# Relative-position attention on Trainium2: half a tile's contents made directly behind the turning of two chunks

## The reference

```python
x = x + 0.5 * ffn(layernorm(x))
x = x + attn(layernorm(x))          # below
x = x + 0.5 * ffn(layernorm(x))

# attn, 16 heads of 16, scale = 1 / sqrt(16)
q, k, v = heads(w @ Wq.T), heads(w @ Wk.T), heads(w @ Wv.T)
rp = heads(sin_table(2 * Lq - 1) @ Wr.T)
AC = einsum('bhid,bhjd->bhij', q + u_bias, k)        # contents
BD = rel_shift(einsum('bhid,hjd->bhij', q + v_bias, rp))   # positions
out = einsum('bhij,bhjd->bhid', softmax((AC + BD) * scale), v)
```

## Time and profile before

| | |
|---|---|
| median of 3 runs | 3118.8 us (3118.35 to 3139.53) |
| the profiled execution's own time | 3117.44 us |
| its span, first to last instruction | 3115.6 us |
| mean granted TensorE clock | 0.959 |
| TensorE matmul busy | 2880.4 us, 92% of the span |
| VectorE busy | 2632.4 us, 84% |
| ScalarE busy | 2497.8 us, 80% |
| GpSimd busy | 2310.7 us, 74% |

### The profile page before, as it was taken

The page is one execution under the profiler, slowest core; times in us unless marked ns, Lnnn a source line. Parts: engine busy times, 40 slices in busy tenths (PEclk is TensorE's granted clock), DMA queues, the critical chain, the costliest instruction groups (busy, mean ns, idle before and its releaser), DMA issues. The chain is left out here.

```text
span 3115.6 us, 110070 instructions
## 1 busy us (share of the span) xinstructions
PE 2880.4 (92%) x40768; PEld 2031.6 (65%) x40768; DVE 2632.4 (84%) x5042; ACT 2497.8 (80%) x3854; POOL 2310.7 (74%) x4135
## 2 busy tenths in 40 slices
PE   6664799999999999999999999999999999999955
PEld 3452377777777777767776777777776777777644
DVE  4663389999989999978998999999998999999966
ACT  3443689898888888978988888888888889888732
POOL 4443888888888888878888888888788888888800
PEclk8886699999999999999999999999999999999977
DMA  6446888888888888878888888888888888888731
GB/s 202 152 130 164 202 216 230 223 232 230 226 221 225 226 229 224 228 201 224 227 227 225 223 232 222 232 225 227 221 229 224 224 225 227 231 224 222 210 123 55
DMA packets 290276, 657.40 MB, mean 211 GB/s; under 512 B 189520, under 2 KB 256976, under 8 KB 272336
## 3 DMA queue, kind: packets, MB, share of 16 engines
q0 software_dynamic: 190960, 526.89, 64.0%
q1 hardware_dynamic: 98784, 123.38, 13.5%
HBM read 77.19 MB, written 46.14 MB: 40 GB/s over the span
## 5 line engine op out<-in xcount | busy, mean ns | idle before, releaser
L826 POOL DMA_DIRECT2D score<-score x3999 | 2178.3, 548 | 498.4 <-ACT score L1065 428.6
L1063 ACT COPY score<-pos_bank 128x512 f32<-128x512 f32 x2048 | 1104.1, 597 | 280.3 <-PE pos_bank L939 277.6
L1073 ACT ACTIVATE score<-score,low 128x1024 f32<-128x1024 f32 x1024 | 1197.0, 1170 | 34.3 <-DVE low L1126 30.3
L1135 DVE COPY prob_t<-pt_bank 128x512 f32<-128x512 f32 x1792 | 1161.8, 684 | 3.0 <-PE pt_bank L1005 2.9
L1005 PEld LDWEIGHTS pt_bank<-ident_sb,score 128*128 128x128 f32 x8192 | 950.0, 142 | 216.5 <-DVE prob_t L1135 46.2
L1005 PE MATMUL pt_bank<-ident_sb,score 128*128 128x128 f32 x8192 | 1083.6, 275 | 7.7 <-ACT score L1073 5.7
L1126 DVE CUSTOM_DVE_ANT_0 score<-ac_bank,score 128x1024 f32<-128x1024 f32 x512 | 627.1, 1225 | 241.3 <-PE ac_bank L991 116.9
L1126 DVE CUSTOM_DVE_ANT_0 score<-ac_bank,score,low 128x1024 f32<-128x1024 f32 x512 | 657.2, 1284 | 55.8 <-PE ac_bank L991 47.3
L939 PE MATMUL pos_bank<-pos,qv 96*32 96x512 bf16 (+15 forms) x12160 | 658.7, 317 | 29.6 <-DMA qv<-qv_parts 25.3
L1019 PE MATMUL acc_bank<-prob_t,vs 128*32 128x128 f32 x16384 | 662.7, 279 | 3.8 <-issue 3.6
L991 PE MATMUL ac_bank<-ks,qu 96*128 96x512 bf16 x2048 | 622.8, 386 | 25.8 <-DVE low L1126 24.4
(11 more groups left out here) (94 smaller groups left out, 867.3 us busy)
## 6 DMA issues: line engine op xcount, KB each, us to landing
score<-score POOLq DMA_DIRECT2D x3937, 129.5 KB, 5.1
pos<-pos_parts SPq DMA_DIRECT2D x96, 128.0 KB, 8.5
qv<-qv_parts SPq DMA_DIRECT2D x192, 64.0 KB, 7.2
ks<-k_parts SPq DMA_DIRECT2D x192, 64.0 KB, 7.1
qu<-qu_parts SPq DMA_DIRECT2D x192, 64.0 KB, 7.2
v_heads<-v_sb SPq DMA_DIRECT2D x8, 1024.0 KB, 6.0
vs<-v_heads SPq DMA_DIRECT2D x32, 256.0 KB, 8.0
pos_parts<-part SPq DMA_DIRECT2D x16, 384.0 KB, 3.7
```

Of the source, the lines that this page charges most:

```text
L826: pool.dma_start(shifted(odd, s, groups, 0), shifted(odd, s, groups, QUAD - 1 - s))\
L1063: act.copy(score[:, at + f, c * BANK:(c + 1) * BANK], ring(m)[:, :]).then_inc(pos_out, 1)
L1073: act.activation(cols, cols, ACT.Exp, bias=low[:, slot(k), NH - 1:NH], scale=-1.0)\
L1135: dve.tensor_copy(prob_t[:, c, :], PT[c % 2][:, :]).then_inc(copied, 1)
```

## The change

In TensorE's body the call of `content` moves from behind the positions to directly behind the two turns, in both half steps. Nothing else is changed: the same contents, of the same tiles, are made in the same half steps, with the same waits.

```diff
@@ -1027,6 +1027,8 @@
                         if there(step, k):
                             turn(step, k, 2 * h)
                             turn(step, k, 2 * h + 1)
+                        if there(step, k + AC_AHEAD + h):
+                            content(step, k + AC_AHEAD + h, 1 - h)
                         weighs = k - 1 + h
                         if there(step, weighs):
                             weigh(step, weighs, 2 - 2 * h)
@@ -1034,8 +1036,6 @@
                         if there(step, n):
                             for m in made_at(k, h):
                                 positions(step, n // FT, m)
-                        if there(step, k + AC_AHEAD + h):
-                            content(step, k + AC_AHEAD + h, 1 - h)
                         if h and k % FT == 1 and group_there(step, fold_no(k)):
                             fold(step, k)
```

## The result

The change makes the kernel slower. Its median is 3186.2 us (4 runs, 3185.5 to 3189.1) against 3123.1 for the kernel before (4 runs, 3118.4 to 3139.5); the ratio is 1.0196, 95% interval 1.0174 to 1.0219. The profiled executions have spans of 3184.4 and 3115.6 us, 68.8 more. The kernel before scatters by 24 us from execution to execution and its profiled one is near the fast end (3117.4), so the difference of the medians is smaller, 63. The forecast was 3204, 87 more than the profiled execution, in a range of 3150 to 3240.

A forecast was written before the change was run, and what follows sets the result against it. TensorE, 99.5% busy, was taken to bound the kernel. Terms of 0.35, 0.30 and 0.07 made 0.72 us a group, 89 us over 124 groups; less 2 for the first tiles, 3117.4 + 87 = 3204 us, range 3150 to 3240.

The forecast's parts named there:

- What bounds: TensorE busy 99.5%, VectorE 91%, both nearly full; TensorE's order is to be read from start to start.
- (1) Neighbours: On TensorE, new neighbours expose the turn's and the fold's loads: 0.35 us a group, bounds -0.055 and 0.75.
- R2: Rival: only the stall costs; the turn's load hides and mode steps alone count; 39 us, 3155; chance 0.10.
- (2) The stall: TensorE's content in half step 5 waits for VectorE's add: 0.30 us a group, bounds 0 and 0.42.
- The chain: VectorE from turn of half step 4 to next content: copies, finish, add, release, 3.66 us; TensorE gets there at 3.36.
- R1: Rival: only the neighbours cost; the add of half step 5 is in time; 52 us, 3167; chance 0.16.
- The spare of 0.11 and 0.17: Time left before the content would wait for the add in other two-copy half steps; 0.17 at first halves.
- R5: Rival, much slower: a longer release eats the spare in other two-copy half steps; 62 us more, 3266; chance 0.14.
- (3) Late rows: Moved rows landing late for the add of half step 4 cost TensorE 0.07 us a group more.
- the new limit of -0.48: Add of half step 4 must start 0.48 us before its turn; a late one, at -0.07, costs 0.41.
- R4: Rival, faster: VectorE gets contents 1 us earlier, ending its waits for them; 46 us less, 3071; chance 0.04.
- Waits of T for copies gone: Sign: the turn on TensorE no longer waits for copies, as in half step 0, worth -0.055 us there.

The follow-up runs named there:

- second experiment: Kernel before with the content only one place earlier, between the weighing and the positions: 3351.1 us, 1.071 of before.
- T P W C: Kernel before with positions ahead of the weighing on TensorE (turn, positions, weighing, content): 3115.8 us, 0.9955 of before.

## Why the prediction was right, and where it was off

*What bounds.* Right: in the quiet groups of both kernels TensorE waits for nothing but the add in half step 5 after the change and, before it, 0.055 for a copy in half step 0; its order is read from start to start.

*(1) Neighbours, forecast 0.35 a group.* Right. 20.99 - 20.37 is 0.62; the stall has 0.27 of it, and 0.35 is left (0.34 in the kernel with the finish behind the add, 20.71 - 20.37). T up to the content takes 0.93, C 0.53, W 0.46, P 0.55, the fold 0.91. The rival R2, that the load hides, is out: what is loaded behind a change counts, and not only how many changes there are.

The Trainium skill ("TensorEngine Tiling (Array Packing)", Key Properties) says that a change of the tiling mode drains TensorE, and gives no cost. The second experiment agrees: with four changes in each half step instead of two the quiet groups cost 260 us more, the exposed loads among them.

*(2) The stall, forecast 0.30.* Right in place and cause, 0.03 too large: the content waits 1.19 less 0.93, about 0.27 (the median over all groups is 1.197 less 0.928). The chain added up to 3.66, and it is 1439.95 - 1436.31 = 3.64; TensorE would have come at 3.37. R1 is out. The spare of 0.11 and 0.17 held in the other half steps (the content comes 0.93 behind the turn in the median of each); R5, that it is eaten, did not come.

*(3) Late rows, forecast 0.07 a group more.* This step failed, even in sign. Above the quiet group there are 0.31 us before and 0.27 after (21.26 - 20.99; 0.24 when added up from turn to turn), where the sum had 0.38. The slack that the longer group gives was sized a little large (0.40; the moves start 25.2 us before the turn, 24.9 before the change, 0.3 earlier). Wrong was what I made of it. I moved the mean of 39 late adds by it and let all 39 pay the whole difference to the new limit of -0.48. But lateness is spread, and the shift puts most of the groups in time. Counted from the starts of adds and turns between 450 and 2880 us, the add of half step 4 starts later than 0.48 before its turn in 62 of 119 groups before the change (a quiet one starts 0.50 before it, so some of these are hardly late) and in 14 of 116 after it; what these 14 are late sums to 6 us, where the forecast had 0.41 x 39, 16 us in 106 groups. VectorE does wait for rows in more places (57 against 39) but only because it is free earlier: in the quiet group the add starts at 1434.60, 1.71 before the turn, so a wait there mostly costs nothing.

The step also took nearly all of the time above the quiet group for late adds of half step 4, and it is not. From turn to turn, between 600 and 2800 us, that time is 32.7 us before and 25.0 after. One pause of each trace has 7.9 and 8.4 of it, the groups with a late add 14.7 and 7.6, and other groups 10.1 and 8.9, for instance where positions stop within an item. With half the moves left out these other groups have only 1 to 2 us, so this part goes with the moves too; by which way is open.

In numbers: 87 forecast, 68.8 in the span. (0.38 - 0.27) x 124 is 14 us, the stall's 0.03 is 4; that is 18 us, about the whole difference. Against the medians, 63 us apart, 6 us more are missing, and they are within the scatter of the kernel before.

*R4, faster,* had its premise fulfilled, 96 us of VectorE's waits for contents gone, and nothing came of it: they turned into waits for turned chunks (115.6 us), because VectorE was not last.

*What was to be seen.* VectorE's busy share: 89% from 600 to 1000, 88% from 1400 to 1800, as said. Adds ahead of the turn: yes. The group of 21.3 to 21.4: 21.26, a little less. "Waits of T for copies gone" can't be read in the list of waits, which names copies for 88.9 us; in the timeline above they are gone, and the turn of half step 0 takes 0.93, as in the others.

## What to carry to other kernels

An order on a full engine has three prices: the gaps and exposed loads at each pair of neighbours, the cover that a moved piece loses for what it waits on, and the time that it gives or takes from transfers further on. Read each from a place in the trace where those neighbours or that chain already occur, here the last tiles. And when slack is shifted against a spread of arrival times, count the cases beyond the limit; a mean of those that are late now says little about who is late afterwards.

## What was not expected of the hardware

With positions ahead of the weighing the two take a little less. In the last timeline of T P W C above it is P 0.44 and W 0.54, 0.98 in all (1509.73 to 1510.17 to 1510.71); with W first, W 0.46 and P 0.55, 1.01 (1506.06 to 1506.52 to 1507.07). The medians over all groups say the same, 0.444 + 0.544 against 0.461 + 0.550. That is 0.02 in a half step and 0.1 in a group. Which of the loads next to the change of pieces makes it was not tried apart.

The step from the 32-column pieces to the full array is dearer than the step there: in the second experiment the content starts 0.58 after a weighing that takes 0.46 when positions follow it, 0.12 more, while the step from the turn to the weighing is 0.09.
